# Two transformer layers on one core: the value products of layer 0 in two halves, with the head sums waiting for each half

## The reference

```python
qkv = jnp.einsum('bnm,fm->bnf', x, Wqkv)
qkv = qkv.reshape(b, n, N_HEADS, -1)
q, k, v = (qkv[..., :dh], qkv[..., dh:2 * dh], qkv[..., 2 * dh:])
scores = jnp.einsum('bnhd,bngd->bnhg', q, k) / SCALE
attn = jax.nn.softmax(scores, axis=-1)
out = jnp.einsum('bnhg,bngd->bnhd', attn, v)
return jnp.einsum('bni,mi->bnm', out.reshape(b, n, -1), Wproj) + bproj
```

## Time and profile before

| what | us |
|---|---|
| median of 3 runs | 2190.77 (2188.96 to 2191.76) |
| the profiled execution | 2186.65 |
| its span, from the first instruction to the last | 2184.9 |
| busy: TensorE 93%, VectorE 81%, ScalarE 72%, GpSimd 49% of the span | 2037.5, 1778.6, 1563.4, 1060.6 |
| the 64 value products of GpSimd | 259.5 |
| granted TensorE clock, mean over the span | 0.975 |

### The profile page before, as it was taken

One profiled execution on the slowest core, in us unless ns is written; L12 is line 12 of the kernel. 1 busy time (PEld: TensorE's weight loads), 2 busy tenths in 40 slices (PEclk: granted clock), 3 DMA queues, 4 the chain that ended last, 5 costly groups with the idle time before them and its releaser, 6 DMA issues. The chain is left out here.

```text
span 2184.9 us, 59761 instructions
## 1 busy us (share of the span) xinstructions
PE 2037.5 (93%) x16112; PEld 1524.8 (70%) x16112; DVE 1778.6 (81%) x5918; ACT 1563.4 (72%) x3951; POOL 1060.6 (49%) x2184
## 2 busy tenths in 40 slices
PE   7999999997999999999999999999999993999990
PEld 5666666664776776676676677677677663999990
DVE  7999999992888888888888888888888884777765
ACT  3666566665888877887887887887878782777774
POOL 6777878783124344334334334434434435444445
PEclk9999999998999999999999999999999996999995
DMA  2000000000000000000000000000200001222227
GB/s 77 23 29 22 29 22 29 24 24 23 2 2 12 2 12 12 4 9 11 7 7 12 9 4 12 12 2 11 89 2 12 12 3 42 64 65 64 67 59 231
DMA packets 63632, 62.84 MB, mean 29 GB/s; under 512 B 9834, under 2 KB 58613, under 8 KB 62855
## 3 DMA queue, kind: packets, MB, share of 16 engines
q1 hardware_dynamic: 54906, 42.64, 6.5%
q0 software_dynamic: 8448, 16.93, 2.2%
HBM read 33.17 MB, written 22.69 MB: 26 GB/s over the span
## 5 line engine op out<-in xcount | busy, mean ns | idle before, releaser
L1368 DVE SCALAR_TENSOR_TENSOR restT<-ps_t,leadT 128x512 f16<-128x512 f32 (+1 forms) x768 | 458.9, 597 | 136.5 <-ACT leadT L1295 106.4
L1295 ACT ACTIVATE leadT<-ps_t 128x512 f16<-128x512 f32 (+1 forms) x768 | 402.2, 524 | 134.4 <-PE ps_t L1169 133.4
L1152 PE MATMUL ps_s<-xT_all,qm 128*128 128x512 f32 (+1 forms) x1024 | 489.9, 560 | 0.8 <-ACT qm L1276 0.8
L1169 PEld LDWEIGHTS ps_t<-ident,p 128*128 128x128 f32 x2560 | 315.4, 141 | 234.0 <-issue 169.4
L1169 PE MATMUL ps_t<-ident,p 128*128 128x128 f32 x2560 | 413.5, 276 | 8.1 <-DVE restT L1368 6.1
L1286 ACT ACTIVATE p<-ps_s,neg_max 128x512 f32<-128x512 f32 (+1 forms) x512 | 325.6, 636 | 80.8 <-DVE neg_max L1358 67.7
L988 POOL CAST v_parts<-v_all 128x36 bf16<-128x36 f32 x256 | 57.3, 224 | 610.2 <-PE ps_o L1183 609.9
L1358 DVE CUSTOM_DVE_ANT_0 ps_s<-ps_s,mask 128x512 f32<-128x512 f32 (+1 forms) x512 | 319.8, 625 | 39.4 <-PE ps_s L1152 38.2
L1152 PEld LDWEIGHTS ps_low<-xT_all,qm 128*128 128x128 f32 x1024 | 194.8, 190 | 135.7 <-issue 122.4
L1143 PE MATMUL ps_qm<-xT_all,m_all 128*128 128x512 f32 x512 | 264.0, 597 | 2.7 <-PEq L766 2.7
L274 POOL TENSOR_TENSOR pv_prod<-probs,kv 128x2048 f32<-128x2048 f32 x64 | 259.5, 4076 | 3.8 <-POOL probs L266 2.3
(11 more groups left out here) (231 smaller groups left out, 4144.2 us busy)
## 6 DMA issues: line engine op xcount, KB each, us to landing
row_in<-rows_dram SPq DMA_DIRECT2D x136, 65.0 KB
y<-results SPq DMA_DIRECT2D x16, 512.0 KB, 5.2
xT<-in_xT SPq DMA_DIRECT2D x32, 128.0 KB, 2.1
xres<-in_xT SPq DMA_DIRECT2D x32, 128.0 KB, 2.1
xT_all<-x2T SPq DMA_DIRECT2D x32, 128.0 KB, 2.0
out_x<-x SPq DMA_DIRECT2D x16, 256.0 KB, 3.4
xT_all<-in_wide SPq DMA_DIRECT2D x1, 2760.0 KB
results<-row_out,row_in POOLq DMA_INDIRECT x136
```

Of the source, the lines that this page charges most:

```text
L1152: mm = pe.matmul(ps_s[n], qm[j][:, n * P:(n + 1) * P], xT_all[:, bass.ds(b * S, (n + 1) * P)], start=True, stop=True)
L1169: mm = pe.transpose(ps_t[g][:, at + n * P:at + (n + 1) * P], probs[i][:, n * P:(n + 1) * P], ident[:, :])
L1295: act.activation(leadT[j][g][:, :], ps_t[g][:, 0:width[g]], ACT.Copy, scale=RAISE)\
L1368: dve.scalar_tensor_tensor(out=restT[j][g][:, :], in0=ps_t[g][:, 0:width[g]], scalar=RAISE, in1=leadT[j][g][:, :], op0=ALU.mult, op1=ALU.s ...
```

## The change

GpSimd's value product of a tile becomes two instructions of 1,024 elements (g = 0 to 7 and 8 to 15), each of which counts pv_multiplied up by one, so the semaphore counts 4 a pair. The first of the two waits for the earlier sums and increments `pool_passed` behind that. `sum_heads` waits for the first half before its first product and for the second before the ninth. `copy_kv` and `normalise` wait for both halves of what they waited for before.

```diff
-    HH = H * H
+    HH, HALF_G = H * H, H // 2
...
-                    when(pool, pv_multiplied, 2 * s)
+                    when(pool, pv_multiplied, 4 * s)
...
-                def pv_products(u, j, a):
+                def pv_products(u, j, a, half):
                     s = 2 * u + j
                     pool.wait_ge(probs_ready, s + 1)
-                    when(pool, pv_summed, 2 * (s - 1) + a + 1)
+                    if half == 0:
+                        when(pool, pv_summed, 2 * (s - 1) + a + 1)
+                        pool.sem_inc(pool_passed, 1)
                     pool.tensor_tensor(
-                        tile(pv_prod, a, HH * DH).rearrange("p (g h d) -> p g h d", g=H, d=DH),
-                        tile(probs, a, HH).rearrange("p (h g) -> p g h", h=H).unsqueeze(3)
-                        .to_broadcast([P, H, H, DH]),
-                        kv[j][:, (2 * a + 1) * P:(2 * a + 2) * P].rearrange("p (g d) -> p g d", d=DH)
-                        .unsqueeze(2).to_broadcast([P, H, H, DH]), ALU.mult).then_inc(pv_multiplied, 1)
+                        tile(pv_prod, 2 * a + half, HALF_G * P).rearrange("p (g h d) -> p g h d", g=HALF_G, d=DH),
+                        tile(probs, a, HH).rearrange("p (h g) -> p g h", h=H)[:, half * HALF_G:(half + 1) * HALF_G]
+                        .unsqueeze(3).to_broadcast([P, HALF_G, H, DH]),
+                        kv[j][:, (2 * a + 1) * P + half * HALF_G * DH:(2 * a + 1) * P + (half + 1) * HALF_G * DH]
+                        .rearrange("p (g d) -> p g d", d=DH)
+                        .unsqueeze(2).to_broadcast([P, HALF_G, H, DH]), ALU.mult).then_inc(pv_multiplied, 1)
...
-                        pv_products(*before(u, j, 1), 0)
-                        pv_products(*before(u, j, 1), 1)
+                        for a in range(2):
+                            for half in range(2):
+                                pv_products(*before(u, j, 1), a, half)
...
-                    pe.wait_ge(pv_multiplied, 2 * s + a + 1)
+                    pe.wait_ge(pv_multiplied, 4 * s + 2 * a + 1)
...
                     for g in range(H):
+                        if g == HALF_G:
+                            pe.wait_ge(pv_multiplied, 4 * s + 2 * a + 2)
                         mm = pe.matmul(tile(ps_oT, a), tile(pv_prod, a * H + g), ident[:, :],
...
-                    when(act, pv_multiplied, 2 * (s - 2) + a + 1)
+                    when(act, pv_multiplied, 4 * (s - 2) + 2 * a + 2)
```

## The result

| | before | after |
|---|---|---|
| median us (6 runs each) | 2189.86 (2186.11 to 2191.76) | 2199.15 (2196.47 to 2201.11) |
| ratio | | 1.0045, 95% interval 1.0033 to 1.0057 |
| span of the profiled execution | 2184.9 | 2196.5 |
| first statistics of pair 2 to those of pair 30 | 63.21 to 494.28 = 431.07 | 63.73 to 506.23 = 442.50 |
| mean step between | 15.40 | 15.80 |

The kernel is slower by 10 us (7.2 to 12.5), as forecast: 2198.3 against a measured 2199.15. In the two profiles the stretch from pair 2 to pair 30 is 11.4 us longer, 0.41 a step; what follows it is the same in both (1690.6 and 1690.3 us).

What follows compares the result with a forecast made beforehand. A loop through GpSimd's value products was taken to set each step; 0.30 + 0.04 - 0.08 = +0.26 us over 30 pairs, less 0.2, gave +7.6 us, median 2198.3. Range 2189.5 to 2203; the forecast's own +4.4 to +11.

Steps and rivals of the forecast that it cites:

- the projection finds TensorE free: TensorE after attnT: with earlier sums the expert product moves ahead of attnT, so the projection need not wait; 0.08 us gained a step.
- the counts: Other engines' waits, counting in fours instead of twos: the same moments as before, costing nothing.
- Step 3: GpSimd's value products: four instructions instead of two cost 0.15 us more a tile, +0.30 a step, bounds 0.02 and 0.39.
- Step 4: GpSimd, between the waits and the first half: the semaphore increment costs 0.04 us for the first tile, nothing for the second.
- Step 5: The other waits, with counts 4s for 2s: same moments as before, nothing; ScalarE's idle time covers copy_kv's later product.
- Step 1: TensorE's sums begun at the half: attnT gains nothing, the projection gains 0.08 us a step, bounds 0 and 0.18.
- Step 2: TensorE's sum_heads: a wait in the middle of the 16 sums adds nothing.
- cheap halves: Rival, GpSimd's products: fixed part 56 ns, increment free; -0.06 us a step, -1.8 us, 2189.0; chance 0.25.
- dearer starts: Rival, GpSimd: each new instruction costs 0.195 us without overlap, increment 0.18; 0.57 a step, 17 us, 2208; chance 0.06.
- the sums are the late chain: Rival, release of attnT: it waits for the sums, not norm2; at most 0.17 us a step gained, 2185.7; chance 0.04.

Runs made afterwards that it cites:

- e1: The kernel before with only the semaphore increment added ahead of each whole value product; ratio 1.0031 to the kernel before.
- e2: The changed kernel, but TensorE waits for both halves of a tile before its first sum; ratio 1.0063 to the kernel before.
- e7: The changed kernel with value products in quarters of 512 elements, TensorE waiting for the whole tile; ratio 1.0146 to the kernel before.
- e4: The changed kernel with ScalarE's norm2 behind copy_oT instead of ahead of it; ratio 0.9975 to the kernel before, 2183.61 us.
- e3: The changed kernel without the semaphore increment before the first half of each tile; ratio 1.0035 to the kernel before.
- e8: The changed kernel with first halves counting a semaphore of their own, pv_multiplied counting whole tiles again; ratio 1.0035 to the kernel before.

## Why the prediction was right, and where its steps were off

The direction and the mechanism held: a loop through GpSimd in which the products stand, and attnT held by ScalarE. e1, e2 and e7 lengthen GpSimd's part, and each lengthens the step by as much while VectorE's wait grows; e4 shows what holds attnT. That 2199.15 lies within 1 us of the 2198.3 is in part luck, as the terms show. Term by term, for the loop's steps:

| term of the sum | forecast | measured |
|---|---|---|
| four instructions for two | +0.30 | +0.29 (8.11 to 8.40) |
| increment | +0.04 | +0.11 (e1, e3) |
| the projection finds TensorE free | -0.08 | -0.08 (e8: L640 3.65/3.72 behind the products, before 3.73/3.80) |
| the counts | 0 | +0.12 (change against e8) |
| a step | +0.26 | +0.44 (15.39 to 15.83) |

- Step 3 was right: e7 shows 0.14 for each further start, where 0.15 a tile was taken and not 0.01.
- Step 4 was too small. The two gaps of the trace, 0.08 and 0.18, differ by about the price of one more command of the sequencer, 0.1 (its records have one register operation in the first and two in the second); I had taken less than half of it.
- Step 5, "the counts of the other waits: the same moments as before, nothing", failed. The moments are the same, but the number must be computed, and where that is done behind the last wait, it is on the path: 0.12 a step (e8), the largest part of what was missing.
- Step 1 was right in its 0.08, but the counts covered it in every second step, so that the change itself shows 3.72 and 3.82.
- Step 2 held: sixteen sums with a wait among them take 1.91 us.

The sum was 0.18 a step short in the loop. The written-out steps, where counts are constants, and the empty end, where attnT gains 0.08 (pair 30 has it 1.98 behind the products for 2.06), bring the stretch to 11.4 against my 7.6, just outside the +4.4 to +11 that I gave the forecast. The difference of the medians, 9.3 us, lies between, and the kernel before, in six runs, has a median 0.9 us under the 2190.77 from which the forecast started; the two bring the time so near to 2198.3. The filling of the pipeline differs by several us between profiles (pair 1's L640 came at 46.9 to 52.6 in these twelve), more than the miss; no kernel has two profiles here, so how much of that is chance is not shown.

Of the signs that I had named, the half product (2132 ns), the 8.40, the unchanged wait ahead of inverse1 and attnT 0.69 behind norm2 came. The steps were to be 15.6 to 15.7 and VectorE's wait up to 0.35; they are 15.73/15.94 and 0.54/0.59. The working also took all steps for one kind, while the loop has two: in the kernel before, L640 comes 3.73 and 3.80 us behind the products by turns. And the lower end of the range, 2189.5, is not the cheap halves' own 2189.0; nothing hangs on that.

The rival of cheap halves fell with e7. That of dearer starts fell with the 8.40 (it had 8.50) and the 0.11 of the increment (it had 0.18), though its 0.57 a step is nearer to the measured 0.44 than my 0.26. The rival in which the sums are the late chain fell with the changed kernel itself, where they lie ready 0.6 us before attnT starts; its price, a kernel 5 us faster, is about what e4 reaches (stretch -4.4, medians -5.8) once ScalarE's chain is out of the way.

## What to carry to other kernels

Splitting a producer pays only if the consumer's start is held by it alone: look at what the released engine has in its queue, and at the distance between its own instructions, before believing the wait that the profile names. On an engine that lies in the loop each further start has to be paid every time, idle share or not. Move what stands in the other engine's queue at the same time; splitting the last piece only was here as fast as splitting both. And look first at how far off the next bound is: here VectorE stood 0.13 to 0.18 us a step behind the loop. When a semaphore's count is rescaled, the sums of the waits may land on the path; a semaphore of its own for the new event avoided that here.

## What the runs showed that I had not expected

- A semaphore increment between two dependent instructions on GpSimd costs 0.10 to 0.12 us.
- A count computed behind a wait costs 0.07 us on GpSimd, and 0.17 us on TensorE with the wait that goes with it.
- Value products of 512 elements take 1155 ns and probs of 512 elements 1061, so the number of elements does not set the time alone. The two differ in the pattern of their operands; no run varies that by itself.
